# Routed experts by dealt blocks of rows in place of all rows through every expert

## The reference

```
x = x + tanh(g_xattn) * attention(layernorm(x), ctx)      # 32 heads of 8, rotary positions, softmax over 256 keys
f = layernorm(x)                                          # 1024 rows of 256
shared = sum over 2 experts of (relu(f @ sw1 + sb1) @ sw2 + sb2) / 2        # hidden width 176
probs  = softmax(f @ router_w + router_b)                 # 32 experts
gates  = the 6 largest of probs in each row, divided by their sum, 0 elsewhere
routed = sum over 32 experts of gates[:, e] * (relu(f @ rw1[e] + rb1[e]) @ rw2[e] + rb2[e])
x = x + tanh(g_ffn) * (shared + routed)
```

## Time and profile before

| what | us |
|---|---|
| runs, median (lowest to highest) | 426.83 (426.57 to 426.93) |
| span of the profiled execution, first to last instruction | 424.8 |
| PE busy | 406.2 (96%) |
| DVE busy | 265.8 (63%) |
| ACT busy | 192.7 (45%) |
| POOL busy | 154.7 (36%) |

### The profile page before, as it was taken

How to read it: one execution, slowest core, us unless ns; L and a number is a source line. 1 busy time by engine, 2 the same in 40 slices (tenths; PEclk the granted TensorE clock), 3 DMA queues, 4 the chain that set the end, 5 groups by cost and what they waited for, 6 DMA issues and landing times.

```text
span 424.8 us, 8222 instructions
## 1 busy us (share of the span) xinstructions
PE 406.2 (96%) x2639; PEld 314.3 (74%) x2639; DVE 265.8 (63%) x530; ACT 192.7 (45%) x372; POOL 154.7 (36%) x297
## 2 busy tenths in 40 slices
PE   7799999999999879999999999999999999999995
PEld 5477766666666557888888888888888888888884
DVE  7987888788787676275555555555555555555554
ACT  4784999979889846232222222222222222222221
POOL 8446333211011125344444333433334344444430
PEclk9999999999999999999999999999999999999999
DMA  7300000000000069499976333343333333332102
GB/s 223 91 2 0 2 2 3 2 2 2 2 0 3 2 184 339 111 236 262 249 216 195 99 99 99 100 99 97 91 96 98 81 103 86 101 92 93 49 0 100
DMA packets 27992, 39.42 MB, mean 93 GB/s; under 512 B 3665, under 2 KB 22145, under 8 KB 27969
## 3 DMA queue, kind: packets, MB, share of 16 engines
q1 hardware_dynamic: 26929, 39.11, 32.8%
q10 hardware_dynamic: 1040, 0.01, 0.1%
HBM read 37.93 MB, written 1.18 MB: 92 GB/s over the span
## 4 chain that ended last, share of the span: by engine, by line
PE 77%; ACT 9%; DVE 8%; issue 3%; DMA 1%; POOL 0%; DVEq 0%; POOLq 0%
PE psum L1296 30%; PE psum L1313 30%; ACT probs L552 5%; PE psum L1096 4%; PE psum L1143 4%; DVE nmax L833 3%; PE psum L997 2%; PE psum L1114 2%; ACT QK L509 1%; PE psum L1203 1%; PE psum L1037 1%; DVE rden L844 1%; ACT QT L558 1%; DVE attn L849 1%; PE psum L1077 1%
## 5 line engine op out<-in xcount | busy, mean ns | idle before, releaser
L678 ACT ACTIVATE hh<-hu 128x512 fp32r<-128x512 f32 x88 | 55.6, 633 | 182.4 <-DVE hu L965 182.4
L965 DVE SCALAR_TENSOR_TENSOR hu<-psum,b1cols,G 128x512 f32<-128x512 f32 x88 | 65.9, 750 | 105.7 <-PE psum L1296 101.7
L833 DVE TENSOR_REDUCE nmax<-psum 128x2 f32<-128x512 f32 x128 | 79.4, 684 | 11.1 <-PE psum L1096 10.4
L552 ACT ACTIVATE probs<-psum 128x512 f32<-128x512 f32 x128 | 69.4, 597 | 12.5 <-PE psum L1114 11.3
L1313 PE MATMUL psum<-hh,w2h 128*128 128x512 f32 x188 | 73.3, 390 | 0.0
L1313 PE MATMUL psum<-hl,w2h 128*128 128x512 f32 x188 | 73.2, 389 | 0.0
L1313 PE MATMUL psum<-hh,w2l 128*128 128x512 f32 x188 | 73.1, 389 | 0.0
L971 DVE SCALAR_TENSOR_TENSOR hl<-hu,hh 128x512 fp32r<-128x512 f32 x88 | 60.9, 694 | 9.1 <-ACT hh L678 9.1
L471 POOL CAST w2h<-w 128x256 fp32r x44 | 18.0, 408 | 125.8 <-PE psum L1313 125.8
L1296 PE MATMUL psum<-xTh,w1h 128*128 128x512 f32 (+1 forms) x188 | 58.1, 390 | 0.0
L1296 PE MATMUL psum<-xTl,w1h 128*128 128x512 f32 (+1 forms) x188 | 57.9, 389 | 0.0
(11 more groups left out here) (150 smaller groups left out, 485.7 us busy)
## 6 DMA issues: line engine op xcount, KB each, us to landing
w<-in_L_ffn_rw_dram SPq DMA_DIRECT2D x8, 1408.0 KB, 9.8
G<-gates_by_expert SPq DMA_DIRECT2D x40, 256.0 KB, 4.0
G<-gates_by_expert SPq DMA_DIRECT2D x8, 448.0 KB, 3.6
G<-gates_by_expert SPq DMA_DIRECT2D x8, 384.0 KB, 3.5
G<-gates_by_expert SPq DMA_DIRECT2D x8, 320.0 KB, 3.6
G<-gates_by_expert SPq DMA_DIRECT2D x8, 192.0 KB, 3.9
x_sb<-in_x_dram SPq DMA_DIRECT2D x4, 256.0 KB, 4.1
G<-gates_by_expert SPq DMA_DIRECT2D x8, 128.0 KB, 4.0
```

The source lines that it names most:

```text
L552: act.activation(probs[g % 2][:, :, n, :], st_bank(g, n)[:, :].rearrange("p (t q) -> p t q", t=TB), ACT.Exp, scale=SCALE).then_inc(exp_ok, 1)
L678: act.activation(hh[(SHT + j) % 2][:, cols], hu[2 * j + half][:, :], ACT.Relu).then_inc(rhh_ok, 1)
L833: dve.tensor_reduce(nmax[i % 2][:, :, n], S_BANK[(4 * i + n) % SB][:, :].rearrange("p (t k) -> p t k", t=TB), AX.X, ALU.max, negate=True). ...
L965: dve.scalar_tensor_tensor(out=hu[2 * (j % 2) + half][:, :], in0=H_BANK[2 * (j % 2) + half], scalar=b1cols[:, bass.ds(it * len(G) + j, 1)] ...
```

## The change

Attention is left as it is, except for the place of some of its last instructions. The routed experts are done on the rows that chose them. A row in memory is 272 float32 numbers (`ROW`): 256 features, the row's number, six expert numbers, six gates, and padding. The 6144 pairs are put in `xd`, a table of 79 blocks of 128 such rows in which each block belongs to one expert; each expert has as many blocks as its rows need, and places not used hold zeros and a row number past the end. 79 is the most that 6144 pairs and 32 experts can need.

- VectorE chooses, ranks and places by batch (`choose`, `gates`, `places`), with counts by TensorE (`counts`); from a batch's ranks follow the places of its rows (`slot`), so that each batch can be dealt before the next is counted.
- GpSimd deals: 48 indirect transfers (8 tiles of 128 rows, 6 choices) write rows of `xrow` to `xd`.
- The shared experts are done first, by rows, in fp32 matmuls and added to `x_sb`.
- SyncE loads the blocks, up to eight ahead. TensorE transposes a block, multiplies it with the first weights of its expert (whose number it reads from a tile into a register), transposes the hidden rows, multiplies with the second weights; ScalarE copies and applies relu; VectorE copies, and multiplies by the gate.
- GpSimd adds each block's 128 output rows to one of two tables in memory by an indirect transfer that accumulates (`yd`, even and odd blocks). A transfer to a table waits until the one before it to that table has landed.
- At the end SyncE loads both tables, VectorE adds them to `x_sb`, SyncE stores.
- During attention SyncE also fills `xd` and `yd` with blanks (11.0 and 2.4 MB) and loads the routed weights.

```
@@ constants @@
+    X_ID, X_EXP, X_GATE = D, D + 1, D + 1 + TOPK
+    ROW = D + 16
+    NB = (TOK * TOPK + NE * (P - 1)) // P
+    SUMS, ROWS_AHEAD = 2, 8
@@ sync @@
-            sp.wait_ge(norm_ok, PAIRS)
...
+            sp.wait_ge(blank_ok, 1)
+            sp.dma_start(xd.rearrange("(n p) c -> p n c", p=P),
+                         blank[:, :].unsqueeze(1).to_broadcast([P, NB, ROW])).then_inc(blank_st, 16)
...
+            sp.wait_ge(dealt, 16 * NT * TOPK)
+            for b in range(NB):
+                r = b % ROWS_AHEAD
+                if b >= ROWS_AHEAD:
+                    sp.wait_ge(xb_mm, b - ROWS_AHEAD + 1)
+                    sp.wait_ge(summed[b % SUMS], 16 * ((b - ROWS_AHEAD) // SUMS + 1))
+                sp.dma_start(xs[r][:, :], xd[b * P:(b + 1) * P, :]).then_inc(xs_ld[r], 16)
...
@@ gpsimd @@
+            for b in range(B):
+                pool.wait_ge(xn2_ok, TB * (b + 1))
+                pool.wait_ge(row_ok, b + 1)
+                pool.wait_ge(slot_ok, b + 1)
+                for n in range(TB * b, TB * b + TB):
+                    for k in range(TOPK):
+                        pool.indirect_dma_start(xd, bass.IndirectOffsetOnAxis(ap=slot[:, n, k:k + 1], axis=0),
+                                                xrow[:, n, :], None).then_inc(dealt, 16)
+            for b in range(NB):
+                i = b % SUMS
+                pool.wait_ge(ob_ok, b + 1)
+                if b >= SUMS:
+                    pool.wait_ge(summed[i], 16 * (b // SUMS))
+                pool.indirect_dma_start(yd[i], bass.IndirectOffsetOnAxis(ap=xs[b % ROWS_AHEAD][:, X_ID:X_ID + 1].bitcast(U32), axis=0),
+                                        ob[i][:, :], None, compute_op=ALU.add).then_inc(summed[i], 16)
@@ scalar, behind attention @@
             second_rows(0)
+            second_rows(1)
+            gate_exponentials(0)
             for t in range(TB):
                 last_transposed_attention(t)
...
+            for b in range(-3, NB):
+                if b + 3 < NB:
+                    block_rows(b + 3)
+                if 0 <= b + 1 < NB:
+                    block_relu(b + 1)
@@ vector, behind attention @@
+            normalised_rows(B - 2)
+            scores(0)
+            scores(1)
+            choose(0)
             for t in range(TB):
                 residual(B - 1, t)
                 row_statistics(B - 1, t)
             variances(3 * TB, TB)
+            gates(0)
+            places(0)
             inverse_deviations(3 * TB, TB)
+            normalised_rows(B - 1)
+            scores(2)
+            for b in range(1, B):
+                if b == 2:
+                    scores(3)
+                choose(b)
+                gates(b)
+                places(b)
...
+            shared_sum(0)
+            shared_sum(1)
+            experts_of_blocks()
+            for n in range(2, NT):
+                shared_sum(n)
...
+            def block_out(b):
+                i = b % SUMS
+                dve.wait_ge(o_mm, b + 1)
+                dve.wait_ge(gate_ok, b + 1)
+                if b >= SUMS:
+                    dve.wait_ge(summed[i], 16 * (b // SUMS))
+                dve.tensor_scalar(ob[i][:, :], Y_BANK[b % 2][:, 0:D], gate[b % 2][:, 0:1], None, ALU.mult).then_inc(ob_ok, 1)
+            for b in range(-2, NB):
+                if b + 2 < NB:
+                    block_hidden(b + 2)
+                if 0 <= b + 1 < NB:
+                    block_gate(b + 1)
+                if b >= 0:
+                    block_out(b)
@@ tensor @@
+            pe.wait_ge(isbe_ok, 1)
+            for c in range(2):
+                ins = pe.matmul(C_B1[c][0:HC, :], rb1_sb[:, c * HC:(c + 1) * HC], is_be[:, :], start=True, stop=True)
+            ins.then_inc(b1_mm, 1)
+            for n in range(2, NT):
+                shared_out(n)
+                if n + 2 < NT:
+                    shared_hidden(n + 2)
+                if n + 1 < NT:
+                    shared_transposed(n + 1)
...
+            def block_transposed(b):
+                for k in range(KD):
+                    ins = pe.transpose(XT_BANK[b % 2][:, k * P:(k + 1) * P], xs[r][:, k * P:(k + 1) * P], ident[:, :])
...
+            def block_first(b):
+                expert[b] = pe.value_load(be_i[0:1, b:b + 1], min_val=0, max_val=NE - 1)
+                for k in range(KD):
+                    ins = pe.matmul(H_BANK[b % 2][:, 0:HID], xT[b % 3][:, k, :], w1[:, k, bass.ds(expert[b] * HID, HID)],
+                                    start=(k == 0), stop=(k == KD - 1))
...
+            def block_second(b):
+                for c in range(2):
+                    rows = HC + c
+                    ins = pe.matmul(Y_BANK[b % 2][:, 0:D], hT[b % 2][0:rows, c, :],
+                                    w2[0:rows, bass.ds(expert[b], 1), c, :].rearrange("p a n -> p (a n)"),
+                                    start=(c == 0), stop=(c == 1))
...
+            pe.wait_ge(shared_ok, NT)
...
+            for b in range(-3, NB):
+                if b + 3 < NB:
+                    block_transposed(b + 3)
+                if 0 <= b + 2 < NB:
+                    block_first(b + 2)
+                if 0 <= b + 1 < NB:
+                    block_hidden_transposed(b + 1)
+                if b >= 0:
+                    block_second(b)
```

More of the change, by code:

```diff
@@ L166, in gated_cross_attention_moe @@
[L166 to L175, removed]
+        v_flat = Vx[:, :, :, :].rearrange("p n h r -> p (n h r)")
@@ L290, in _ @@
                              sw1.rearrange("e (k p) h -> p k e h", p=P)[:, k]).then_inc(ws_ld, 16)
+            sflat1 = sb1.rearrange("e h -> (e h)")
+            for t in range(SHT):
+                rows = P if t < SFULL else SREST
+                sp.dma_start(b1s[0:rows, t:t + 1], sflat1[t * P:t * P + rows].rearrange("(p a) -> p a", a=1)).then_inc(ws_ld, 16)
             sflat2 = sw2.rearrange("e h n -> (e h) n")
@@ L304, in load_second @@
[L304 to L333, removed]
-                if r in (9, 11):
-                    load_second(1, (r - 9) // 2)
@@ new lines, in shared_relu @@
+            def shared_relu(n):
+                act.wait_ge(st2_mm, n + 1)
+                if n == 0:
+                    act.wait_ge(ones_ok, 4)
+                if n >= 2:
+                    act.wait_ge(so_mm, n - 1)
+                for t in range(SHT):
+                    rows = P if t < SFULL else SREST
+                    ins = act.activation(hsT[n % 2][0:rows, t, :], SHT_BANK[n % 2][0:rows, t * P:(t + 1) * P], ACT.Relu,
+                                         bias=b1s[0:rows, t:t + 1])
+                ins.then_inc(hsT_ok, 1)
@@ new lines, in _ @@
+            for n in range(SUMS):
+                i = (NB + n) % SUMS
+                for b in range(B):
+                    rows = slice(TB * b, TB * b + TB)
+                    dve.wait_ge(sum_ld[i][b], 16)
+                    if n:
+                        dve.wait_ge(sum_ok, B * (n - 1) + b + 1)
+                    else:
+                        dve.wait_ge(shared_ok, NT)
+                    dve.tensor_tensor(res[:, rows, :], x_sb[:, rows, :], acc[:, i, rows, :], ALU.add).then_inc(sum_ok, 1)
@@ L1300, in result @@
[L1300 to L1315 removed]
+            router_scores(2)
@@ new lines, in _ @@
+            shared_transposed(0)
+            counts(1)
+            shared_out(0)
+            shared_hidden(2)
+            shared_transposed(1)
+            counts(2)
+            shared_out(1)
+            shared_hidden(3)
+            shared_transposed(2)
+            counts(3)
+            pe.wait_ge(later_ok, 1)
+            pe.matmul(C_BE, every[:, :], later[:, :], start=True, stop=True).then_inc(be_mm, 1)
+            pe.wait_ge(isbe_ok, 1)
+            for c in range(2):
+                ins = pe.matmul(C_B1[c][0:HC, :], rb1_sb[:, c * HC:(c + 1) * HC], is_be[:, :], start=True, stop=True)
```

749 lines of the change are left out of this document (394 added, 355 removed).

## The result

The changed kernel takes 447.02 us (median of three runs, 445.68 to 447.99) against 426.83: a ratio of 1.047, 95% interval 1.0453 to 1.0487, slower. I had said 415 and faster. The profiled execution took 447.99 us, with a span of 446.2.

A forecast was written before the change was run, and what follows sets the result against it. TensorE's routed matmuls were taken to bound the kernel. The sum was 217 to the first block + 4 filling + 179.4 blocks + 12 end = 412.4 us of span, 414.4 as run time, said as 415; range 392 to 472.

The forecast's parts named there:

- the first block: Start of the routed blocks: dealing and shared rows both end near 215 us, blocks start at 217.
- filling: Start of the block stage: about 4 us to fill the pipeline.
- the end: After the blocks: last scatter 1.0 + 2.4, table loads 4.1, additions and last store some 4.5: 12 us.
- the scatter chain, (1.65 + L) / 2: Block stage: product 0.45, issue 1.0, landing L 2.4, semaphores 0.2, shared by two tables: 2.03 us a block.
- Rival 1: Block stage: the scatter's landing decides above L = 2.95 us; slower, 459 us at L = 4.1; chance 0.28.
- TensorE's term: Block stage: 2.05 us of work plus 0.25 for register read and waits, 2.3 us a block, deciding.
- Dealing: Before the blocks: 48 indirect transfers on GpSimd at 1.0 us from 162.5, ending at 210.5 us.
- Rival 2: Before the blocks: dealing dearer, 438 us at 1.5 us a transfer, break-even at 1.26; chance 0.13.
- half speed: Dealing under the VectorE-GpSimd port lock: some 13 transfers through by 190 us, 35 follow, time about 429 us.
- Shared rows: Shared experts on TensorE before the blocks: 15.2 us of work behind one stop near 193.5, ending at 214.5.
- Rival 3's milder half: TensorE at 1.2 GHz for shared work: blocks start near 230, time 428 us; whole rival's chance 0.09.
- the blanks and weights: During attention: 13.4 MB of blanks and 11.5 MB of weights move in 116 us, which just fits.

The follow-up runs named there:

- e2: Changed kernel with one table and one product buffer in place of two: 613.26 us (one run).
- e8: Changed kernel with two tables kept and twelve buffers of rows in place of eight: 445.68 us.
- e5: Changed kernel with three tables in place of two and nine buffers of rows in place of eight: 405.84 us.
- e10: Changed kernel with one table, scatters storing in place of adding, so the sum over a row's experts is left out: 521.66 us (one run).
- e9: Changed kernel with four tables in place of two and twelve buffers of rows in place of eight: 406.28 us.
- e6: Changed kernel with three tables, nine buffers and shared rows reordered, two tiles between one batch's counts and the next: 405.45 us.
- e1: Changed kernel with four tables in place of two, still eight buffers of rows: 422.27 us.

## Why the prediction was wrong

The sum was 412.4 us of span; the span is 446.2, 33.8 more. By its own terms: the first block at 230.7 in place of 217.0, 13.7; filling 6.0 in place of 4, 2.0; 78 blocks at 2.498 in place of 2.3, 15.4; the end 14.6 in place of 12, 2.6, of which 1.8 are the last transfer (5.22 in place of 1.0 + 2.4).

**The blocks: the step that failed is the scatter chain, (1.65 + L) / 2.** Its form was right, and two things in it were mis-sized. One table's turn is 2 x 2.498 = 5.00 us in place of 4.05. Of the 0.95 between, 0.56 is the issue: it was priced like a dealing transfer, 1.0, and an adding one takes 1.56. Another 0.20 is the hand-over from landing to product and from product to issue: 0.40 in the chain, where I had 0.2 for two semaphores. The landing, of which I was least sure, was nearly right: 4.11 - 1.56 = 2.55 behind the issue with two in flight, 2.2 when alone, against my 2.4, so 0.15. The product gives the rest, 0.04. That is 2.498 a block, above the 2.46 that I gave as the point from which the kernel is slower than before.

Rival 1 (chance 0.28) is what happened in its sign, `ob` waiting for a transfer, and not in its reason: the landing stayed under the 2.95 from which it was to decide. e2, e8 and e5 show the turn. e10 shows that adding costs 0.60 of issue and 0.56 to 0.80 of landing; that it is dearer because it reads first no run shows.

**TensorE's term was too high.** I took 2.05 of its own and 0.25 for waits and the register read. In e9, with no wait left, a block is 1.905 in all. No stop for the register read can be seen there; only where rows come late does the weight load that follows it (L1459) show waits put down to "issue". So the 2.3 was wrong to the other side: with three tables, late as the start still is, the forecast's 415 is undercut by 9 us.

**Dealing: the price was low.** 1.29 us from start to start against 1.0 makes 61.7 us of dealing in place of 48, and it began 1.6 us later than the 162.5 assumed. Rival 2 broke even at 1.26, so its price came true, just. Its sign did not, since the blocks started at 230.7 and waited for the shared rows, and its reason did not. While GpSimd dealt, VectorE's step of 384 elements with two inputs took 0.56 us, where I had worked out 0.57, and GpSimd's issues took 0.96 us each but for five of 1.10 to 1.26, all of them up to 202, while VectorE chose and placed: 1.3 us in all. The Trainium skill ("SBUF — State Buffer", section "SBUF: two separate sides") has descriptors held up while VectorE runs an operation in a 2-port mode, and by the same section lets a step with two inputs block only a GpSimd operation that reads SBUF. The prediction left these conditions out, and its half speed is its own. In this trace those 1.3 us are the most that the lock can be, where half speed would have been some 14.

**Shared rows: the order was not followed through.** They were to end at 214.5 and end at 230.1. I had TensorE stop once, for `experts_of_blocks`, and VectorE wait 0.5 us a batch for counts. In fact TensorE stops in every batch, by the ring of waits shown above, and VectorE waits 3.9 to 5.5. So TensorE goes on behind `experts_of_blocks` at 206.65 in place of 193.5: 13 of the 15.6 us. That e6 ends them at 213.4 is partly luck, as it does more of them ahead of the stop.

With the waits came the lower clock: four matmuls at L1374 take 1.43 us at the full level and 2.55 to 2.69 between 168 and 212. A tile of shared work (L1395 to L1386) takes 5.91 us in place of 3.08, and three such tiles stand in the way (from 179, 192 and 207), so the clock is some 8.5 us of the 15.6 by an estimate from these rows. Rival 3's milder half is thus part of the start, though ahead of the stop more than behind it. Without it the first block would still have waited for dealing, to 229.6. The Trainium skill ("TensorE: Matmul & The Clock Gate", Part 1) has the clock fall when the engine idles; here, unlike in the earlier trace rows, a run shows it: 0.64 and 0.62 where TensorE is busy 12.24 and 14.56 of 25 us, and 1.00 again from 215.

**What the chances missed.** They left the sign open, 0.48 for faster against 0.48 for slower. Rivals 1 and 2 were priced one at a time, each with the rest at its forecast, and each came out just past its own break-even: 2.498 against 2.46, and 1.29 against 1.26. By the forecast's sum the measured blocks alone make 430 us and the measured start alone 428; together they make 443.5, and filling and end add 4.6. The two rivals depend on one unknown, what an indirect transfer costs GpSimd, and should have shared one chance.

What held: attention unchanged, and the blanks and weights, which are out of the way before the blocks begin.

## What to carry to other kernels

A resource used in turn, such as a table that each transfer must leave before the next may enter, needs (its whole turn) / (the work between) copies: here 4.64 / 1.91 = 2.4, so three. The third, with its product buffer, was worth 41 us (447.02 to 405.84) where the work of every engine stayed as it was, and made the change 5% faster than the kernel before. Then check the ring that feeds it: a buffer freed by the landing belongs to the same turn, and a fourth table with too short a ring lost 16 us of it again. When two paths end within a microsecond of each other, an experiment on either alone says that it doesn't matter; change both once before you believe it.

## What the runs showed of the hardware

- In these runs an indirect transfer of 128 rows keeps GpSimd 0.96 us, an accumulating one 1.56 us, each with at least 0.30 us to the next. In the kernel after, beside VectorE's routing steps, five of 48 took 1.10 to 1.26.
- The last scatter takes longer, the more tables there are: 3.73 us from issue to landing with one table (e2), 5.22 and 4.50 with two (after, e8), 6.23 with three (e5), 7.75 and 6.91 with four (e1, e9). This eats part of the gain at the end (14.6, 17.1 and 19.1 us with two, three and four tables, loads of the tables included). The last transfer in the chain of the kernel after, and then of the run with four tables and eight buffers:

```profile
431.59 5.22 DMA sum<-ob,xs
```

```profile
398.43 7.75 DMA sum<-ob,xs
```

Whether it is the loads of the finished tables or the scatters before it that hold the last one up was not tried.
